# A decoder layer on one core: the second group's attention placed later, four record writes two and two, a weight copy earlier, and eleven more identity products

## The reference

```python
h = x @ Wh + bh                                   # block 1: linear attention, 16 heads of 8
q = sigmoid(x @ Wq + bq); k = sigmoid(x @ Wk + bk); v = x @ Wv + bv
attn = (q @ (k^T v)) / (q @ sum(k))               # per head
out = relu((layernorm(attn) * ln_w + ln_b) * (h + beta) @ Wo + bo)

q = x @ Wq; k = ctx @ Wk; v = ctx @ Wv            # block 2: softmax attention, 16 heads of 64
out = softmax(q k^T / 8) v @ Wo + bo

logits = x @ gate_w; e = argmax(logits)           # block 3: shared FFN, and one of 8 experts
out = swiglu(x, shared) + swiglu(x * sigmoid(max logit), expert e)
```

## Time and profile before

| what | value |
|---|---|
| median of three runs | 604.29 us |
| the profiled execution's own time | 604.9 us |
| its span (first to last instruction) | 603.2 us |
| mean granted clock of TensorE | 0.993 |
| PE busy | 576.2 us (96%) |
| DVE, ACT busy | 432.7 and 432.1 us (72%) |
| POOL busy | 306.9 us (51%) |

### The profile page before, as it was taken

The page is one execution under the profiler, slowest core; times in us unless marked ns, Lnnn a source line. Parts: engine busy times, 40 slices in busy tenths (PEclk is TensorE's granted clock), DMA queues, the critical chain, the costliest instruction groups (busy, mean ns, idle before and its releaser), DMA issues.

```text
span 603.2 us, 15181 instructions
## 1 busy us (share of the span) xinstructions
PE 576.2 (96%) x5479; PEld 529.2 (88%) x5479; DVE 432.7 (72%) x1214; ACT 432.1 (72%) x1514; POOL 306.9 (51%) x328
## 2 busy tenths in 40 slices
PE   7978999999999999999999999999999999999993
PEld 7867998998999899988899898988998988899893
DVE  3868666878686768766877777676857459689773
ACT  2668778777876777676867687768776876777771
POOL 3544653365336743475256544563365336246774
PEclk9998999999999999999999999999999999999998
DMA  7530000000000000010000000000040021252530
GB/s 153 136 76 14 18 2 1 15 19 2 1 15 28 28 2 14 19 33 6 14 20 26 11 2 15 19 19 2 24 136 20 7 65 37 68 144 80 151 101 15
DMA packets 24955, 23.52 MB, mean 39 GB/s; under 512 B 7007, under 2 KB 22497, under 8 KB 24880
## 3 DMA queue, kind: packets, MB, share of 16 engines
q1 hardware_dynamic: 21520, 15.96, 10.1%
q0 software_dynamic: 2784, 6.32, 3.0%
q10 hardware_dynamic: 576, 0.26, 0.6%
HBM read 15.03 MB, written 7.95 MB: 38 GB/s over the span
## 4 chain that ended last, share of the span: by engine, by line
PE 67%; ACT 16%; DVE 10%; DMA 3%; issue 2%; POOL 1%; SPq 1%; POOLq 0%; DVEq 0%
PE bank L1451 8%; PE bank L1429 8%; PE bank L1416 8%; PE bank L1440 8%; PE bank L1277 7%; ACT prob L1147 7%; PE bank L1279 6%; PE bank L1278 6%; PE bank L1565 4%; PE bank L1295 2%; PE bank L1397 2%; PE bank L1582 2%; ACT probT L1153 2%; PE bank L1283 2%; ACT L1118 1%
## 5 line engine op out<-in xcount | busy, mean ns | idle before, releaser
L1147 ACT ACTIVATE prob<-bank,mneg 128x128 f32<-128x128 f32 x512 | 183.3, 387 | 65.1 <-DVE mneg L866 64.9
L604 POOL TENSOR_TENSOR prob<-prob,rden 128x512 f32<-128x512 f32 x124 | 126.6, 1041 | 102.7 <-DVE rden L873 102.6
L1147 ACT ACTIVATION_READ_ACCUMULATOR prob<-bank,mneg 128x1 f32 x512 | 115.3, 225 | 0.0
L1153 ACT COPY probT<-bank 128x512 f32<-128x512 f32 x128 | 77.6, 608 | 16.3 <-PE bank L1429 15.6
L866 DVE TENSOR_REDUCE mneg<-bank 128x4 f32<-128x512 f32 x128 | 83.0, 670 | 2.7 <-PE bank L1416 2.5
L1429 PE MATMUL bank<-ident,prob 128*128 128x128 f32 x512 | 78.4, 276 | 1.8 <-ACT probT L1153 0.7
L543 POOL TENSOR_TENSOR rstd<-var_eps,neg_half 128x4 f32<-128x4 f32 x24 | 24.7, 1030 | 99.1 <-DVE var_eps L700 99.1
L1429 PEld LDWEIGHTS bank<-ident,prob 128*128 128x128 f32 x512 | 59.8, 142 | 8.4 <-issue 2.9
L1416 PE MATMUL bank<-kT,qT 64*128 64x128 f32 x1024 | 65.9, 279 | 0.0
L1416 PEld LDWEIGHTS bank<-kT,qT 64*128 64x128 f32 x1024 | 59.8, 188 | 5.8 <-issue 2.5
L1451 PE MATMUL bank<-xwo,oT 128*128 128x128 f32 x512 | 63.7, 277 | 0.4 <-issue 0.4
(11 more groups left out here) (225 smaller groups left out, 1391.3 us busy)
## 6 DMA issues: line engine op xcount, KB each, us to landing
prob<-routed SPq DMA_DIRECT2D x39, 128.5 KB, 2.3
s_work<-in_x_dram SPq DMA_DIRECT2D x8, 256.0 KB, 2.9
ctx_nat<-in_ctx_dram SPq DMA_DIRECT2D x8, 192.0 KB, 2.6
routed<-blank SPq DMA_DIRECT2D x9, 128.5 KB, 3.5
s_work<-in_L_ffn_rt_gate_dram SPq DMA_DIRECT2D x1, 1024.0 KB, 5.5
s_work<-in_L_ffn_rt_up_dram SPq DMA_DIRECT2D x1, 1024.0 KB, 9.5
prob<-in_L_xattn_Wq_dram SPq DMA_DIRECT2D x1, 512.0 KB, 6.8
xwo<-in_L_xattn_Wo_dram SPq DMA_DIRECT2D x1, 512.0 KB, 9.7
```

Source lines behind the costliest of these rows:

```text
L604: nc.gpsimd.tensor_tensor(view, view, spread(rden[:, m % 2, c * NC:(c + 1) * NC], 2, S), ALU.mult)\
L1147: last = nc.scalar.activation(prob[:, m % 2, p * S:(p + 1) * S], score_bank[c][:, i * S:(i + 1) * S], ACT.Exp, bias=mneg[:, m % 2, p:p + 1 ...
L1153: nc.scalar.copy(probT[:, m % 2, c * 512:(c + 1) * 512], made(r1, ("T", m, c))[:])\
```

## The change

Five edits:

1. In `MOVED`, group 1's "x^T low" (DVE) goes from (-2, 3) to (-1, 0), behind two row maxima. Its "sigmoids" go behind all exponentials of batch 0, and all that follows of block 1 goes 1 to 5 beats later: "k^T v" to (0, 0), "q k^T v" and "attention" to (0, 1), "turn gated" to (1, 0), "output" and "x1" to (1, 1), "turn x1" to (1, 3).
2. The high part of the shared gate and up weights is copied at (-2, 2) instead of (-1, 2) (ACT), and the low part made at (1, 2) instead of (-1, 3) (DVE). An exponential of four numbers behind the first high part of x1^T has ACT load that table there.
3. "scatter 0" and "scatter 1" both stand behind step 10's `write_out`, "scatter 2" and "scatter 3" both behind step 11's.
4. ACT copies the first tile's expert weights ahead of its last copy of turned probabilities, instead of behind it.
5. `stay_awake`: 8 becomes 11, 9 becomes 12, and 5 are new ahead of (-2, 0).

```diff
-                 (1, "turn x"): (-2, 3), (1, "copy x^T"): (-2, 3), (1, "x^T low"): (-2, 3),
+                 (1, "turn x"): (-2, 3), (1, "copy x^T"): (-2, 3), (1, "x^T low"): (-1, 0),
...
+                 (1, "sigmoids"): (-1, 3), (1, "k^T v"): (0, 0), (1, "mask"): (0, 0), (1, "q k^T v"): (0, 1),
...
-        POOL_TAIL = {1: ["rstd"], 7: ["record"], 10: ["scatter 0"], 11: ["scatter 1"], 12: ["scatter 2"],
-                     13: ["scatter 3"]}
+        POOL_TAIL = {1: ["rstd"], 7: ["record"], 10: ["scatter 0", "scatter 1"], 11: ["scatter 2", "scatter 3"]}
...
-                    if (n, b) == (-1, 3):
+                    if (n, b) == (1, 2):
                         dve.wait_ge(wm_hi, 1)
...
                     nc.scalar.copy(xn2T_hi[:, g % 2], made(r1, (g, 12))[:]).then_inc(hi_in[1], 1)
+                    if g == 0:
+
+                        nc.scalar.activation(table_first[:], neg_half[:], ACT.Exp)
...
-                    if (n, b) == (-1, 2):
+                    if (n, b) == (-2, 2):
                         act.wait_ge(wm_in, 16 * 4)
                         nc.scalar.copy(sh_gu_hi[:], rawgu).then_inc(wm_hi, 1)
+                    if (n, b) == (B - 1, NC - 1):
+                        act.wait_ge(table, TABLE_1)
+
+                        act.wait_ge(s_ready, 4 * (B - 2))
+                        act.wait_ge(wr_in, 16 * 3)
+                        held[0] = weights_of(0)
+                        copy_weights(0)
...
-                        stay_awake(8)
+                        stay_awake(11)
+                    if (n, b) == (-2, 0):
+                        stay_awake(5)
...
-                        stay_awake(9)
+                        stay_awake(12)
```

More of the change, by code:

```diff
@@ L347, in decoder_layer @@
                  (1, "stats of x"): None, (1, "rstd of x"): (-4, 2), (1, "normalise x"): (-4, 3),
-                 (1, "turn x"): (-2, 3), (1, "copy x^T"): (-2, 3), (1, "x^T low"): (-2, 3),
+                 (1, "turn x"): (-2, 3), (1, "copy x^T"): (-2, 3), (1, "x^T low"): (-1, 0),
                  (1, "project first pair"): (-1, 0), (1, "first pair"): (-1, 0),
-                 (1, "project second pair"): (-1, 1), (1, "second pair"): (-1, 1)})
+                 (1, "project second pair"): (-1, 1), (1, "second pair"): (-1, 1),
+                 (1, "sigmoids"): (-1, 3), (1, "k^T v"): (0, 0), (1, "mask"): (0, 0), (1, "q k^T v"): (0, 1),
+                 (1, "attention"): (0, 1), (1, "gate terms"): (0, 0), (1, "rstd of attention"): (0, 1),
+                 (1, "gating, first half"): (0, 2), (1, "gating, second half"): (0, 2),
+                 (1, "turn gated"): (1, 0), (1, "copy gated^T"): (1, 0), (1, "output"): (1, 1), (1, "x1"): (1, 1),
+                 (1, "rstd of x1"): (1, 1), (1, "normalise x1"): (1, 1), (1, "turn x1"): (1, 3),
+                 (1, "x1^T high"): (1, 3), (1, "x1^T low"): (1, 3)})
         def steps_at(table_, starts, n, b):
@@ L1168, in empty_qk, with weights_of, copy_weights @@
                                ps[:].rearrange("p (k n) -> p k n", k=2)).then_inc(r1.emptied["act"], 1)
+            def weights_of(j):
+                if j == ROUND1:
+                    act.wait_ge(table, TABLE_2)
+                half, i = (0, j) if j < ROUND1 else (1, j - ROUND1)
+                return load_one(mybir.EngineType.Activation, gu_tab[0:1, half, i:i + 1], (E - 1) * 2 * I)
+            held = {}
+            def copy_weights(j):
+                if j >= 3:
+                    act.wait_ge(gu_ready, j - 2)
+                nc.scalar.copy(w4[j % 3], rt_gu[:, bass.ds(held.pop(j), 2 * I)])
+                if j + 1 < TILES:
+                    held[j + 1] = weights_of(j + 1)
             bc = lambda v: v.partition_broadcast(P)
@@ L1226, in _ @@
                             ffn(g, step)
-            def weights_of(j):
-                if j == ROUND1:
-                    act.wait_ge(table, TABLE_2)
-                half, i = (0, j) if j < ROUND1 else (1, j - ROUND1)
-                return load_one(mybir.EngineType.Activation, gu_tab[0:1, half, i:i + 1], (E - 1) * 2 * I)
-            held = {}
-            def copy_weights(j):
-                if j >= 3:
-                    act.wait_ge(gu_ready, j - 2)
-                nc.scalar.copy(w4[j % 3], rt_gu[:, bass.ds(held.pop(j), 2 * I)])
-                if j + 1 < TILES:
-                    held[j + 1] = weights_of(j + 1)
-            act.wait_ge(table, TABLE_1)
-            act.wait_ge(s_ready, 4 * (B - 2))
-            act.wait_ge(wr_in, 16 * 3)
-            held[0] = weights_of(0)
-            copy_weights(0)
             empty_PV(B - 1, 0)
```

## The result

| | median, us | runs | lowest to highest |
|---|---|---|---|
| kernel before | 604.14 | 18 | 603.05 to 605.06 |
| changed kernel | 605.02 | 18 | 604.65 to 606.72 |

The ratio is 1.0024, with a 95% interval from 1.0016 to 1.0032: slower by 1.0 to 1.9 us. It is not the ratio of the two medians, which lie 0.88 us apart; the means lie 1.40 apart. The forecast was 603.6, no measurable change. 605.02 lies in the outer range of 600.9 to 605.9, but above the forecast's own range of 602.6 to 604.9, and the change has the other sign. The profiled execution of the changed kernel took 604.99 us with a span of 603.3, against 604.9 and 603.2 before.

The account below looks back on a forecast made before the run. PE, busy 96% of the span, was taken as the bound. Head +1.0 and tail -1.65 made -0.65, put on the median 604.29: 603.6 us; range 600.9 to 605.9, the forecast's own 602.6 to 604.9.

Parts of the forecast that it names:

- the head's term, +1.0: Head up to batch 2's first turning: the middle of +1.9 and +0.1 us, bounds -1.95 and +3.6.
- a second fall: Rival: clock falls again at 73 to 76 us, losing 1.7; head +3.6, time 606.3 us; chance 0.17.
- priced at nothing: Moved shared-weight parts and table load in the head: nothing, at most 0.7 us.
- If the clock holds: No fall behind the first pause: "output" at 66.0, batch 2's first turning at 74.5 us, +0.1.
- the case with a fall: Clock falls behind the first pause: "output" at 67.7, batch 2's first turning 76.2 against 74.34 us, +1.9.
- put at 0.6: A held clock at the first pause of the kernel before would bring little there, 0.6 us.
- The wait for a v bank: Near 57 us PE waits 1.4 us, from 56.5 until the next v product gets its bank at 57.9.
- The chain behind it: From "output" to batch 2's first turning: 8.5 us against 6.1 of PE work, so PE waits some 2.4.
- -1.65 forecast: Tail: earlier record writes remove PE's waits for tiles 21 and 22; -1.65 us, bounds -1.8 and 0.
- +0.1 forecast: Eleven more identity products on PE cost +0.1 us in all, between 0 and +2.0.
- The chain was not covered: Rival: "output" by 65.9 us leaves no wait behind it; head -1.0, tail -2.65, time 601.6; chance 0.40.
- The tail did give its gain: Rival: tile loads wait for something other than records, so the tail gives nothing; 605.3 us; chance 0.10.

Follow-up runs that it names:

- edit 3 alone, set 3: Kernel before with only the four record writes placed two and two; 601.92 us (5 runs), ratio 0.9961 to the kernel before.
- edit 3 alone, set 1: Kernel before with only the four record writes placed two and two, tail with further waits; 619.36 us, ratio 1.0010 to the kernel before.
- edit 5 alone, set 1: Kernel before with only the eleven more identity products, tail with further waits; 618.88 us, ratio 1.0006 to the kernel before.
- edit 3 alone, set 5: Kernel before with only the four record writes placed two and two; 602.22 us (6 runs), ratio 0.9962 to the kernel before.
- edit 2 alone, set 4: Kernel before with only the moved shared-weight parts and early exponential, tail with further waits; 619.70 us, ratio 1.0004 to the kernel before.
- edits 2 and 4, set 1: Kernel before with only the moved shared-weight parts, early table load and earlier first-tile weight copy, tail with further waits; 620.09 us, ratio 1.0027.
- edit 1 alone, set 1: Kernel before with only the second group's steps moved, tail with further waits; 620.95 us, ratio 1.0052 to the kernel before.
- edit 1 alone, set 4: Kernel before with only the second group's steps moved, tail with further waits; 622.03 us (6 runs), ratio 1.0051 to the kernel before.
- changed, products at "turn x1": Changed kernel with 7 identity products ahead of group 1's "turn x1", none in the first pause; 604.90 us, ratio 1.0010 to the kernel before.
- edits 2 to 5: Changed kernel with the second group's steps back where they were; 603.08 us, ratio 0.9983 to the kernel before.
- edits 2 to 5 with products: Changed kernel with the second group's steps back, plus 8 identity products in the pause ahead of "k^T v"; 602.86 us, ratio 0.9976 to the kernel before.
- the one with steps a beat sooner: Changed kernel with group 1's "turn gated" to "turn x1" a beat sooner; 606.58 us, ratio 1.0043 to the kernel before.
- without edit 2: Changed kernel with only DVE's low part of the shared weights back at (-1, 3), tail with further waits; 620.96 us, ratio 1.0039 to the kernel before.

## Why the prediction was wrong

**The positions.** All from PE's timelines, in us from group 0's "output":

| kernel, profiled execution | clock low | turning | PV |
|---|---|---|---|
| before | 45 to 49 | 47.97 | 51.30 |
| edit 3 alone, set 3 | 46 to 50 | 48.00 | 51.31 |
| edit 3 alone, set 1 | 46 to 49 | 47.30 | 50.63 |
| edit 5 alone, set 1 | 46 to 49 | 47.31 | 50.63 |
| edit 3 alone, set 5 | no fall | 47.01 | 50.33 |
| edit 2 alone, set 4 | 44 to 48 | 48.72 | 52.00 |
| edits 2 and 4, set 1 | no fall | 47.62 | 50.91 |
| edit 1 alone, set 1 | no fall | 48.57 | 52.15 |
| edit 1 alone, set 4 | 46 to 50 | 49.91 | 53.49 |
| changed | 74 to 78 | 48.90 | 53.67 |
| changed, products at "turn x1" | no fall | 48.91 | 52.36 |
| edits 2 to 5 | 46 to 50 | 48.16 | 51.44 |

**The step that failed is the head's term, +1.0, taken as the middle of two cases with at most one fall.** From group 0's "output" to tile 0 it measured +2.29. Of this 0.93 are waits ahead of the turning, and 1.3 is the fall from 74.6 on, behind the waits for "turn x1" and the turning, which the sum left out as a rival ("a second fall") at 0.17. That the 0.93 are so near to the +1.0 is luck. The clock held in the first pause, and for that case the forecast said +0.1; edit 1 brought +0.60 (47.97 to 48.57), and edit 2, priced at nothing, brought 0.33 more.

**"If the clock holds" also set unlike executions against each other**: the changed kernel with the clock held against the kernel before with a fall. Compared alike, edit 1 costs 1.94 at the turning with a fall at the first pause in both (47.97 to 49.91; 2.61 from the executions at 47.30) and 1.56 with none in either (47.01 to 48.57). Either is above the +1.0; the +1.9 of the case with a fall was right to 0.04. What the kernel before loses by a fall, put at 0.6, was 0.97 to 1.0 where it began within "k^T v" and 0.3 where it began 1 us later (47.30 and 47.31 against 47.01). And the sum, worked out against the profiled execution with its fall, was put on the median, 0.6 lower; against that execution it stood at 604.2 to 604.3.

**The second fall was not a rival at 0.17 but the case.** The rival had its place, 73 to 76, and its mechanism right, but sized it at 1.7; it cost 1.3. What stood against it, that idle time of 1.95 us behind 54.66 had left the clock at 1.00, was one execution: edits 2 to 5 with products had a fall at 57, in just that stretch. Its condition was wrong: "output" later than about 67.5. "output" stood 40.06 behind group 0's, which is 66.4 in the kernel before's time, and the clock fell all the same. It fell at 74 in both profiled executions of the changed kernel. Of the other executions with edit 1 and without products, one had no fall, two had one at 46, and the one with steps a beat sooner had two. The changed kernel's 28 runs (18 and 10) never had a mean clock above 0.992, while the undisturbed profiled executions without a fall in the head had 0.993 to 0.996, so each seems to have had at least one. That the upper heap has two is what its lower mean clock, mostly 0.989, and its 1.5 us speak for; none of its runs was profiled, so this is not shown.

**Edit 2 was not nothing.** I priced the low part by the row of an x1 addition, 0.69, whose operand is in PSUM. The operation's own row in the kernel before was there and I hadn't read it:

```profile
47.58 1.33 DVE L1049 TENSOR_TENSOR sh_gu_lo<-x,sh_gu_hi 128x512 fp32r<-128x512 f32 x1
```

It works beside POOL, and one of the two waits for the other. With DVE first, beside POOL's second pass in the changed kernel, it took 0.72. In the changed kernel POOL's second pass waits 0.33 and the turning with it (48.57 to 48.91 without a fall); with edit 1 absent, DVE's pass takes 0.93 longer (0.72 to 1.65), and edit 2 costs 0.6 to 0.9 at the turning (47.01 to 47.62 without a fall, 48.00 to 48.72 and 47.31 to 48.16 with one), for all that "attention" starts 0.47 sooner without the pass ahead of it (21.00 against 21.47, no fall in either). This accounts for a part of what edit 3 alone brings, 2.3 to 2.4, above the 1.0 of edits 2 to 5; the interval of the latter is 0.5 to 1.5, so the rest stays open. The Trainium skill, page "SBUF — State Buffer", section "Who interferes with whom", says that a DVE instruction with two inputs in SBUF and a GpSimd instruction that reads SBUF exclude each other, and that the later one waits for the whole of the other. The rows agree to 0.2: POOL's pass starts 0.46 ahead of the end of DVE's (72.11 and 72.57) and takes 0.33 more where DVE was first, and DVE's ends 0.56 behind POOL's where POOL was first.

**What was right.** The pause at 45 with POOL as its releaser (45.5 forecast, 44.97 measured). "attention" with the clock held at 52.5 forecast, 51.86 measured. The wait for a v bank with a fall was 1.4 in the forecast and 1.36 in edit 1 alone, set 4, released by DVE's low part of the context as forecast; with the clock held it is 0.16. "output" without a fall 66.0, measured 65.78, which with the earlier start is 0.4 later than forecast; with a fall 41.33 behind group 0's (67.7 - 26.37), measured 41.39 (67.36 - 25.97). The chain behind it was put at 8.5 and measured 8.51 without edit 2 and 8.84 with it. Two waits there, both released by POOL.

**Edit 3**: -1.65 forecast. From tile 0 to the end the trace gives -1.5 (77.3 to 75.8) and, with edit 3 alone, -1.75 (600.4 - 524.85 = 75.55). PE's waits for tiles 21 and 22 went, as forecast. The times gave 2.4 and 2.3, with intervals of 1.6 to 3.1 and 1.4 to 3.3; whether more than the tail is in it stays open. **Edit 5** cost nothing, +0.1 forecast; **edit 4**, whose place is just ahead of tile 0, gave 0.1 at most: from `PV` of batch 1 to tile 0 PE takes 448.23 before and 448.15 after.

**The sum as it should have been.** Against the profiled execution: head with waits +0.9 (edit 1 +0.6, edit 2 +0.3), the fall from 74.6 on +1.3 and 0.1 of small waits between, tail -1.65: +0.7, where the two traces give +2.29 - 1.54 = +0.75. A fall behind the first pause too, if the upper heap is that, a third of the runs, adds an estimated 0.4 (1.3 / 3). That is 1.1 us, against 1.0 to 1.9 measured; runs of the kernel before without a fall would account for more, but how many there are is not shown.

**The rivals.** The chain was not covered; 8.5 us are fixed by rows, and this should have weighed more than the chance of 0.40 that it got. The tail did give its gain.

## What to carry to other kernels

When a disturbance such as a fall of the clock comes and goes between executions, compare like with like: price the change once with it in both kernels and once in neither, and never take the middle of a mixed pair. Price a moved operation from its own row, at its old place, and look what POOL does at the new one. A wait that is moved is still a wait, and a pause of PE also brings the chance of a fall behind it. Identity products in both long pauses of the changed kernel gave back 1.9 us at no cost, since PE had nothing else to do there; with one pause filled, a fall still came behind smaller waits in one version.

## What the runs showed of the hardware

- The same kernel (edit 3 alone) with the same pause of 2.02 us kept the clock in one execution and fell to 1.2 GHz behind it in another; likewise edit 1 alone. One fall cost 0.3 to 1.3 us: at the first pause of the kernel before 1.0, and 0.3 where it began 1 us later, and 1.3 with edit 1. The page "TensorE: Matmul & The Clock Gate" of the Trainium skill, Part 1, says of the clock's first rise that it varies from run to run of the same kernel; these traces show the like of a fall.
- Of four profiled versions with products in the first pause alone, one had the fall behind the next waits instead, of 0.36 to 0.66 us (at 57, in edits 2 to 5 with products).
- One DVE operation, the low part of the shared weights, took 0.72, 1.33 or 1.65 us in the three traces shown, and a POOL pass 1.04 or 1.37, each longer where it started behind an operation of the other engine.
- In two sets the tail of all kernels was 14 us longer, with PE waiting for ACT in the tail's loop. Why is open; one chip showed it in one set and not in another.
